# Root lookup in a graph layer: two accumulating products of 49 columns in place of one of 98

## The reference, cut to what matters

```python
deg = jnp.maximum(jnp.zeros((n,), x.dtype).at[dst].add(1.0), 1.0)
edge_weight = (deg[src] * deg[dst]) ** (-DEG_POWER)          # DEG_POWER = 0.5
edge_msg = jax.nn.relu(edge_attr @ W1e + b1e) @ W2e + b2e
messages = (x[src] + edge_msg) * edge_weight[:, None]
agg = jax.ops.segment_sum(messages, dst, num_segments=n)
...
h = jax.nn.relu(combined @ W1n + b1n) @ W2n + b2n
out = h + x
```

## Time and profile before

| | before |
|---|---|
| median of 3 runs | 1180.37 us (1178.91 to 1180.9) |
| the profiled execution | 1182.25 us, span 1180.5 us, mean granted clock 0.99 |
| PE / PEld busy | 1017.4 / 803.1 us, 12051 instructions each |
| DVE busy | 1066.5 us, 4594 instructions |
| ACT / POOL busy | 712.2 / 789.0 us |

### The profile page before, as it was taken

One profiled execution on the slowest core, in us unless ns is written; L12 is line 12 of the kernel. 1 busy time (PEld: TensorE's weight loads), 2 busy tenths in 40 slices (PEclk: granted clock), 3 DMA queues, 4 the chain that ended last, 5 costly groups with the idle time before them and its releaser, 6 DMA issues. The chain is left out here.

```text
span 1180.5 us, 34517 instructions
## 1 busy us (share of the span) xinstructions
PE 1017.4 (86%) x12051; PEld 803.1 (68%) x12051; DVE 1066.5 (90%) x4594; ACT 712.2 (60%) x1313; POOL 789.0 (67%) x790
## 2 busy tenths in 40 slices
PE   0333899999999999999999999999999999999986
PEld 0332677777777777777777777777777777777753
DVE  7799899999999999999999999999999999999458
ACT  6852566565665656656566565665656656566535
POOL 1044777777777777777777777767677676776365
PEclk9999899999999999999999999999999999999989
DMA  6034444444444444444444444444444444442363
GB/s 224 8 144 131 123 113 113 130 117 125 114 112 129 117 123 118 113 125 117 124 118 113 125 117 121 116 110 120 114 121 119 108 118 115 124 116 71 116 246 123
DMA packets 60617, 143.21 MB, mean 121 GB/s; under 512 B 16819, under 2 KB 24550, under 8 KB 60064
## 3 DMA queue, kind: packets, MB, share of 16 engines
q1 hardware_dynamic: 35504, 88.35, 24.3%
q0 software_dynamic: 23936, 49.45, 18.2%
q10 hardware_dynamic: 1008, 3.21, 0.8%
HBM read 134.36 MB, written 6.57 MB: 119 GB/s over the span
## 5 line engine op out<-in xcount | busy, mean ns | idle before, releaser
L1037 POOL DMA_INDIRECT arena<-node_rows,idx x748 | 745.8, 997 | 283.3 <-issue 170.6
L1205 ACT ACTIVATE arena<-bank 128x686 f16<-128x686 f32 x432 | 393.1, 910 | 368.7 <-PE bank L1111 368.7
L1260 DVE TENSOR_SCALAR arena<-iota_c,code 128x343 f16<-128x343 f16 x864 | 303.5, 424 | 0.0
L1122 PE MATMUL bank<-t_words,arena 128*126 128x256 f16 x2352 | 298.6, 274 | 0.4 <-DVE arena L1328 0.4
L1111 PE MATMUL bank<-arena 128*128 128x343 f16 x864 | 223.5, 340 | 64.8 <-ACT arena L1205 41.7
L1276 DVE SCALAR_TENSOR_TENSOR arena<-iota_h,hi_f,bank 128x98 f32<-128x98 f32 x864 | 223.0, 311 | 58.5 <-PE bank L1076 58.5
L1122 PEld LDWEIGHTS bank<-t_words,arena 128*126 128x126 f16 x2352 | 251.2, 136 | 1.1 <-issue 0.8
L1197 ACT ACTIVATE arena<-bank 128x512 f32<-128x512 f32 (+1 forms) x432 | 226.6, 571 | 35.4 <-PE bank L1063 32.8
L1063 PE MATMUL bank<-w1e,arena 64*128 64x128 f32 x3264 | 223.2, 273 | 0.0
L1063 PEld LDWEIGHTS bank<-w1e,arena 64*128 64x128 f32 x3264 | 219.1, 191 | 3.9
L1246 DVE TENSOR_SCALAR arena<-arena,part_f 128x258 f16<-128x258 uint8 x432 | 185.5, 465 | 0.8 <-DVE t_words L627 0.6
(11 more groups left out here) (199 smaller groups left out, 867.7 us busy)
## 6 DMA issues: line engine op xcount, KB each, us to landing
arena<-in_attr SPq DMA_DIRECT2D x48, 512.0 KB
arena<-in_attr SPq DMA_DIRECT2D x48, 448.0 KB
arena<-low_src SPq DMA_DIRECT2D x50, 293.6 KB, 5.8
arena<-node_rows,idx POOLq DMA_INDIRECT x748
arena<-in_attr SPq DMA_DIRECT2D x48, 128.0 KB
node_rows<-arena SPq DMA_DIRECT2D x1, 3160.5 KB, 8.9
arena<-in_x ACTq DMA_DIRECT2D x7, 448.0 KB, 11.4
arena<-in_x SPq DMA_DIRECT2D x6, 512.0 KB, 13.9
```

The lines of the kernel that those rows point to most:

```text
L1037: nc.gpsimd.indirect_dma_start(out=edge_rows[:, u, j, 0:ROW], out_offset=None, in_=table, in_offset=bass.IndirectOffsetOnAxis(ap=idx[:, c, ...
L1122: mm = nc.tensor.matmul(x_sum[0:XC, 0:2 * D], strip[:, u, k, :], T16[:, k, :], start=k == 0, stop=k == NBLK - 1)
L1205: nc.scalar.activation(strip[:, u, :, 2 * p * W:2 * p * W + 2 * W].rearrange("p k (t w) -> p t k w", t=2), pair_bank[:, :].rearrange("p (t ...
L1260: ins = nc.vector.tensor_scalar(code_oh[:, p % PB, j, :, 0:W], iota_c[:, :].rearrange("p (k w) -> p k w", w=W), code[:, column(c), 2 * p + ...
```

## The change

The lookup takes two products for a tile: the one-hot with the 49 high parts, and the same one-hot with the 49 low parts, accumulated into the same 49 columns of PSUM. The pick then reads 49 columns. `iota_h` has 49 numbers, and the scratch output `picked` is half as wide.

```diff
-        iota_h = sb("iota_h", [128, LK])
+        iota_h = sb("iota_h", [128, NBLK])
...
-        loop.picked = take(4 * LK)
+        loop.picked = take(4 * NBLK)
...
-            numbers(iota_h[:, :], [[0, 2], [1, NBLK]])
+            numbers(iota_h[:, :], [[1, NBLK]])
...
-                        at = (2 * (k - first) + j) * LK
-                        mm = nc.tensor.matmul(look_ps[:, at:at + LK], low_t[:, (c * UL + k) % RL, j * 128:(j + 1) * 128], s_parts[:, :],
-                                              start=True, stop=True)
+                        at = (2 * (k - first) + j) * NBLK
+                        for part in range(2):
+                            mm = nc.tensor.matmul(look_ps[:, at:at + NBLK], low_t[:, (c * UL + k) % RL, j * 128:(j + 1) * 128],
+                                                  s_parts[:, part * NBLK:(part + 1) * NBLK], start=part == 0, stop=part == 1)
                 mm.then_inc(looked, 1)
...
-                    at_slot, at = slice(2 * k + j, 2 * k + j + 1), (2 * (k % 2) + j) * LK
+                    at_slot, at = slice(2 * k + j, 2 * k + j + 1), (2 * (k % 2) + j) * NBLK
                     ins = nc.vector.scalar_tensor_tensor(
-                        out=loop.picked[:, at:at + LK], in0=iota_h[:, :], scalar=hi_f[:, column(c), at_slot],
-                        in1=look_ps[:, at:at + LK], op0=ALU.is_equal, op1=ALU.mult, accum_out=s_d[:, u, at_slot])
+                        out=loop.picked[:, at:at + NBLK], in0=iota_h[:, :], scalar=hi_f[:, column(c), at_slot],
+                        in1=look_ps[:, at:at + NBLK], op0=ALU.is_equal, op1=ALU.mult, accum_out=s_d[:, u, at_slot])
```

## The result

The changed kernel takes 1167.43 us (median of 4 runs, 1166.52 to 1168.03) against 1179.84 us before: a ratio of 0.9895, 95% interval 0.9881 to 0.991. The forecast was 1165.2 us with a range of 1160.5 to 1182. The gain is 12.4 us where 15.2 were forecast.

A forecast was written before the change was run, and what follows sets the result against it. Bound: a path alternating between PE and DVE. 47 steps x 0.305 us = 14.3, with the prologue 15.2 us: 1182.25 to 1167.0 us, less 1.9 for the profiled run, 1165.2 us; range 1160.5 to 1182.

The forecast's parts named there:

- A PE leg and a DVE leg set the step: Edge pass: each 21.07 us step is 14.39 us of PE work, then 6.68 us of DVE work.
- The picks: DVE: each pick 51 ns shorter; only 8 of 18 in a step count, 0.41 us off.
- The products: PE lookup: 25 ns per 49-column product with its load, 7.5 ns more a tile, 14 tiles, 0.105 us a step.
- The rest: Everything else in the step, including the spreading products behind PE's eight lookup products: no wait, queue or DMA added.
- The second cycle: PE's path through ACT's copy: about 20.64 us a step, becoming 20.75, just under the first path's 20.77.
- Two signs: PE's 0.43 us wait for DVE shrinks to about 0.3; wrong if it is gone and another wait stands there.
- DVE's waits for the lookup: DVE waiting for PE's lookup over the edge pass: would grow from 58 to some 87 us.
- The first lookups: Before step 0, all 18 picks count, 51 ns each: 0.9 us off, once.

The follow-up runs named there:

- e9: Kernel before, with the change applied only to pairs 2 to 5, the other five pairs keeping 98 columns: 1161.27 us, ratio 0.9848 to the kernel before.
- e12: Kernel before, with two products of 49 columns side by side and the pick still reading 98: 1186.34 us, ratio 1.0056 to the kernel before.
- e4: Changed kernel, with the last product of each lookup 98 columns wide: 1480.77 us, ratio 1.0017 to the kernel before (1478 us there).
- e3: Changed kernel, with each tile's second product sent to columns of its own: 1478.96 us, ratio 1.0007 to the kernel before (1478 us there).
- e8: The changed kernel itself, run again on the chips where the kernel before took 1478 us: 1483.38 us, ratio 1.0041 to the kernel before.
- e2: Kernel before, with one product of 98 columns and a pick of only the 49 high parts: 1500.18 us, ratio 1.0142 to the kernel before.
- e5: Changed kernel, with only one product of 49 columns for a tile: 1499.12 us, ratio 1.0168 to the kernel before (1478 us there).
- e6: Kernel before, with the change applied only to pairs 2 to 5, first run: 1472.89 us, ratio 0.9965 to the kernel before (1478 us there).

## Why the prediction was right, step by step

- *A PE leg and a DVE leg set the step.* Shown by e9 to e12: each step came within 0.01 us of the sum of legs, with the growth of the PE leg taken from the changed kernel's trace.
- *The picks*: 51 ns forecast, 50 measured; the DVE leg 0.41 us forecast, 0.42 measured.
- *The products*: taken as 25 ns between bounds of 22 and 42.5, measured 25 to 26 (a lookup of eight takes 0.204 us at the median of 37 steps, one of four products of 98 took 0.171). So a tile costs 8.2 ns more, and not 7.5. Both the choice between columns and load, and the small allowance over the columns, held; that the allowance was just 3 ns was a guess. The Trainium skill's floor of about 25 ns from start to start ("TensorE: Matmul & The Clock Gate", "Wait — 56ns, not 53.3ns?") agrees: by columns alone it would be 22 ns, and 49 columns took 25. No run here tells a floor from a small fixed price of a product and its load. The 81 ns at 128 columns that the Trainium skill's same page gives for a stream of load and product pairs ("Back-to-back issue gap") does not agree: such pairs stand 25 ns apart at 49 columns and 42.5 ns at 98.
- *"The rest" was mis-sized*: the spreading products behind the lookup were named and costed at nothing. They lost cover for their first load: 1.56 us for 1.54, three times in the PE leg, 0.05 us a step. With it the leg's 0.105 us become 0.155, and the measured leg grew by 0.15. That it is the cover of this load is what e4 shows. It makes 47 x 0.05 = 2.4 us, nearly all of the 2.8 us by which the gain fell short.
- *The second cycle* lay further off than forecast. PE's wait for DVE was read as the 0.43 us that the timeline marks as idle, but that is counted from the end of the product before, and a product that follows without a wait starts before that end. From start to start, the sixteen products of L1063 and the next counting product stand 0.99 us apart where PE waits for nothing (in the changed kernel 624.51 to 625.50). At the place where PE waits for DVE they stood 626.36 - 624.87 = 1.49 us apart:

```profile
624.87 1.05 PE L1063 MATMUL bank<-w1e,arena 64*128 64x128 f32 x16
```

  They now stand 617.62 - 616.57 = 1.05 us apart. By the medians over the pass (0.986, 1.484 and 1.054 us) DVE held PE by 0.50 us, and still holds it by 0.07. The weight loads of that product tell the same (waits from 120 to 1100 us: in total, times, longest; before, then after):

```profile
PEld bank L1111 <- DVE arena L1260: 28.4, 46, 0.6
```

```profile
PEld bank L1112 <- DVE arena L1261: 8.7, 46, 0.2
```

  The wait for DVE is there in 46 steps of both. The second cycle was thus 21.06 - 0.50 = 20.56 us and not 20.64, and is 20.81 - 0.07 = 20.74 now, which its 14 tiles and four exposed loads explain (0.115 + 0.06). The two legs, at 21.07 - 0.42 + 0.155 = 20.81 us, remain the bound.
- *Two signs.* The text said that this wait would shrink to about 0.3 us. By its own two cycles, 20.77 and 20.75, it had to shrink to 0.02; it took the shortening of the step for that of the wait. It also said that it would be wrong if PE's wait for DVE were gone and another stood in the step. In the timeline's brackets the wait is gone, but by the starts and the loads it is not; and the wait for ACT that is left (0.63 us) stood there before (0.67).
- *DVE's waits for the lookup*: about 87 us forecast from 120 to 1100 us, 86.5 measured there.
- *The first lookups*: 0.9 us forecast. From PE's first lookup to its first counting product it is 104.96 - 93.70 = 11.26 us instead of 105.93 - 93.74 = 12.19, 0.93 less.

The profiled executions differ by 14.2 us (1182.25 to 1168.03), more than the medians. Part of this is no effect of the edit. In the windows from 106 to 124 us and from 124 to 144 us the granted clock was 0.79 and 0.93 in the trace of before, and 1.00 in both in the trace of after and in those of e9 to e12. From the first counting product to the first turning product the trace of before takes 147.67 - 105.93 = 41.74 us; e12, whose picks are as wide and whose PE has more to do, takes 145.68 - 105.41 = 40.27 us. So this one trace of before is some 1.5 us too long there. From the first turning product to the last the changed kernel gains 11.4 us, which is 45 steps of 0.25. With the 0.93 us of the first lookups this comes to about the 12.4 us of the medians. A single pair of traces gives the steps well, the total less well.

## What to carry to other kernels

When two engines wait for each other in every step, draw the cycle through both and price an edit only where it stands in it: the same shorter pick was worth 51 ns in two phases and nothing in three, while its price on the other engine was due in four of the five, in 14 of 18 tiles. Apply such a trade pair by pair, not to the whole loop. A shorter instruction on PE also uncovers the weight load behind it; cost the instruction that follows, too. And read how long an engine was held from start to start: idle time that is counted from the end of an overlapping instruction comes out too short, here 0.43 us for 0.50, and none for 0.07.

## What the hardware showed unexpectedly

A weight load of 128 contiguous 16-bit columns hides behind a product of 49 columns at the full clock: 25 ns for load and product together. A load of 126 columns does not: the next load follows it by some 55 ns, of which 14 show behind a product of 98 columns and 29 behind one of 49. Two products in a row that add to the same columns stand as close as two that do not, 25 ns (the changed kernel and e3). In the first lookups, where four products of 98 columns took 0.49 us and not 0.34, eight of 49 took 0.49 us too (at 96.92 in the changed kernel), so there the second load and product cost nothing that the rows show.

Signals from PE to the other engines came late in e8 (by 2.3 us after the recorded end of the product at the pick shown), and PE halted with nothing to wait for, while a pick lasted as long as ever (262 ns). On the two chips where this was so the kernel before took 1478 us instead of 1180; why is open. There the changed kernel was 0.4% slower than the kernel before (e8), and e2 and e5, which only take work away, 1.4 and 1.7% slower: a verdict on a trade of tenths of a microsecond holds only where the handoffs are as quick as in the trace on which it was worked out. Only e6, the edit that changes no more than the DVE leg needs, was faster there too (0.9965, 0.9942 to 0.9987).
